# A two-layer graph network on one core: the second layer's preparation in new order, with an unused bf16 product ahead of each s product

## What is computed

```python
h = jnp.maximum(_layernorm(x), 0.0)
q, k, v = h @ Wq.T + bq, h @ Wk.T + bk, h @ Wv.T + bv
scores = jnp.where(adj > 0, q @ k.T / sqrt(128), neg)
x = x + jax.nn.elu(jax.nn.softmax(scores, axis=-1) @ v)

node = jnp.maximum(_layernorm(x), 0.0)
h = node @ W
s1, s2 = h @ a[:128, 0], h @ a[128:, 0]
e = jax.nn.leaky_relu(s1[:, None] + s2[None, :], negative_slope=0.01)
att = jax.nn.softmax(jnp.where(adj > 0, e, NEG_INF), axis=1)
x = x + h + att @ node
```

## Time and profile before

| | |
|---|---|
| median of three runs | 757.64 us (757.02 to 760.74) |
| profiled execution | 758.56 us, its span 756.7 us |
| mean granted TensorE clock | 0.977 |
| busy share: TensorE, VectorE, ScalarE, GpSimd | 95%, 74%, 72%, 59% |
| chain that ended last | TensorE's strip products 27%, ScalarE's signs 2.6%, one DMA 1.6% |
| layer one's last product of weights and v ends | 477.8 us |
| first strip of layer two starts | 510.9 us |

### The profile page before, as it was taken

How to read it: one execution, slowest core, us unless ns; L and a number is a source line. 1 busy time by engine, 2 the same in 40 slices (tenths; PEclk the granted TensorE clock), 3 DMA queues, 4 the chain that set the end, 5 groups by cost and what they waited for, 6 DMA issues and landing times. The chain is left out here.

```text
span 756.7 us, 18309 instructions
## 1 busy us (share of the span) xinstructions
PE 715.2 (95%) x6243; PEld 605.8 (80%) x6243; DVE 559.7 (74%) x1190; ACT 545.0 (72%) x1090; POOL 449.7 (59%) x388
## 2 busy tenths in 40 slices
PE   7989999999999999999999998759699999999996
PEld 5567888888888888888888787758588888888885
DVE  6977787887878788787878876679387477577572
ACT  4745877778687777878777787767986897887810
POOL 6687799999999999999999989480000000000000
PEclk9998999999999999999999999979899999999998
DMA  6289999998988889898888943963244342442100
GB/s 236 99 288 217 246 278 239 271 260 251 259 236 282 244 265 254 251 268 231 284 249 254 247 112 71 130 108 100 63 84 85 83 96 63 94 92 64 38 10 13
DMA packets 193307, 132.71 MB, mean 175 GB/s; under 512 B 174064, under 2 KB 180720, under 8 KB 184944
## 3 DMA queue, kind: packets, MB, share of 16 engines
q1 hardware_dynamic: 192528, 131.90, 65.7%
q10 hardware_dynamic: 576, 0.26, 0.1%
q0 software_dynamic: 160, 0.00, 0.0%
HBM read 71.31 MB, written 18.89 MB: 119 GB/s over the span
## 5 line engine op out<-in xcount | busy, mean ns | idle before, releaser
L770 ACT ACTIVATE scores<-scores,neg_max 128x1024 f32<-128x1024 f32 x128 | 146.0, 1142 | 50.5 <-DVE neg_max L904 50.5
L917 DVE TENSOR_TENSOR low<-scores 128x1024 bf16<-128x1024 f32 x96 | 138.1, 1438 | 39.2 <-ACT scores L770 39.2
L1171 PE MATMUL spare<-v_parts,hiT 128*128 128x256 bf16 x768 | 160.8, 273 | 0.0
L350 POOL TENSOR_SCALAR mask_both<-mask_bytes 128x2048 bf16<-128x2048 uint8 x64 | 153.2, 2394 | 5.4 <-POOL mask_bytes L345 0.4
L898 DVE CUSTOM_DVE_ANT_0 scores<-ps_s,mask_both 128x1024 f32<-128x1024 f32 x128 | 155.9, 1218 | 0.2 <-issue 0.2
L345 POOL TENSOR_SCALAR mask_bytes<-adj_both 128x2048 uint8<-128x2048 int32 x64 | 148.2, 2334 | 3.2 <-DMA adj_both<-in_adj 2.3
L1167 PE MATMUL spare<-v_parts,lowT 128*128 128x128 bf16 x768 | 144.1, 220 | 1.9 <-DMA lowT<-low 1.8
L784 ACT ACTIVATE hiT<-spare 128x512 bf16<-128x512 bf16 (+1 forms) x128 | 102.5, 801 | 39.2 <-PE spare L1141 36.7
L1605 PE MATMUL ps_x<-q_parts,over_k 128*128 128x258 bf16 x1024 | 117.0, 275 | 5.2 <-issue 4.0
L1605 PEld LDWEIGHTS ps_x<-q_parts,over_k 128*128 128x128 fp8e4 x1024 | 99.5, 98 | 20.7 <-issue 5.5
L1106 PE MATMUL ps_s<-k_hi,q_strip 128*128 128x512 f32 x256 | 112.6, 440 | 2.0 <-PEq L81 1.9
(11 more groups left out here) (174 smaller groups left out, 1274.4 us busy)
## 6 DMA issues: line engine op xcount, KB each, us to landing
adj_both<-in_adj SPq DMA_DIRECT2D x64, 1024.0 KB, 5.3
mask_bytes_dram<-mask_bytes SPq DMA_DIRECT2D x32, 512.0 KB, 2.8
x_sb<-in_x SPq DMA_DIRECT2D x8, 256.0 KB, 6.7
out<-res SPq DMA_DIRECT2D x32, 64.0 KB, 1.6
lowT<-low SPq DMA_TRANSPOSE x96, 4.8
mask_both<-s_row_dram SPq DMA_DIRECT2D x1, 1024.0 KB, 7.3
mask_both<-s_row_dram SPq DMA_DIRECT2D x1, 768.0 KB, 12.1
over_k<-mask_bytes_dram SPq DMA_TRANSPOSE x16, 4.6
```

The costliest lines, as they stand in the source:

```text
L350: return nc.gpsimd.tensor_scalar(out, src, -NEG, NEG, ALU.mult, ALU.add)
L770: nc.scalar.activation(sc, sc, ACT.Exp, bias=neg_max[:, bn:bn + 1], accum_out=row_sum[:, bn, k:k + 1]).then_inc(exp_done, 1)
L917: nc.vector.tensor_tensor(low[k][:], p, high_half(p), ALU.subtract).then_inc(low_done, 1)
L1171: last = nc.tensor.matmul(ps_a[:], high, v_parts[:, t, :, :], start=first, stop=final)
```

## The change

The diff does the following; only the end of the second block and the start of the third differ.

- `PIECES`: the tiles are prepared in nine pieces instead of eight chunks, the last two of two tiles each.
- GpSimd's `normalise` stands between its epilogues in another way: chunks 0 to 2 one strip later, 3 in the last one, 4 and 5 behind the last epilogue. VectorE takes the inverse root of tiles 24 to 29 and normalises them before the last epilogues are in, and does the same for 30 and 31 alone behind the last strip. In the last strip its low halves are made in another order.
- TensorE's s product of piece 0, the turn of piece 2 and the s1 product stand behind the strip's loop. Each s product of a tile has a product in front that nothing reads: `ident_half` (bf16 128 x 128) by 256 columns of `v_parts`, written to free columns of the s product's bank. There is a second s1 product (for strips 4 to 7), the order of hW products and turns is another, and the last three hW products stand behind `top_b`.
- ScalarE weighs nothing any more; VectorE weighs v1[0] of all chunks, GpSimd v1[1] of chunks 0 to 2 (`weigh_low`), and VectorE v1[1] of 3 to 7 at the start of the third block, where GpSimd splits them (`low_split`, for which strip 0 waits). VectorE makes the early signs of pieces 1, 3 and 5.
- SyncE issues the second `load_mask` before both `store_s1`; these hold chunks 2 to 4 and 5 to 7.
- The signs of group 1 are made from the second s1 product, 8 of them on VectorE (`VECTOR_SECOND`) and 24 on ScalarE, which waits for both transfers only for group 2. `add_last_hw` stands behind group 0.

The diff, cut to its core (indentation shortened):

```diff
+PIECES = [slice(4 * c, 4 * c + 4) for c in range(NC - 1)] + [slice(T - 4, T - 2), slice(T - 2, T)]
+NP2 = len(PIECES)
...
+def split_words(pool, c, i):
+halves = chunk(v1[i], c).bitcast(BF16)
+return nc.gpsimd.tensor_tensor(halves[:, :, 0::2], chunk(v1[i], c), halves[:, :, 1::2], ALU.subtract)
+def weigh_words(c, i):
+return nc.vector.scalar_tensor_tensor(out=v1[i][:, 4 * c:4 * c + 4, 0:D], in0=chunk(h_sb, c), scalar=0.0,
+                              in1=v1[i][:, 4 * c:4 * c + 4, D].unsqueeze(2).to_broadcast([D, 4, D]),
+                              op0=ALU.max, op1=ALU.mult)
...
-BY_SCALAR = (3, 4, 5, 6)
-S1_CHUNKS = (slice(1, 4), slice(4, NC))
+FIRST, MIDDLE, LAST = slice(0, 24), slice(24, 30), slice(30, 32)
+BY_VECTOR = (1, 3, 5)
+LOW_EARLY = 3
+S1_CHUNKS = (slice(2, 5), slice(5, NC))
...
+def pieces_till(c):
+return c + 1 if c < NC - 1 else NP2
...
 for b in range(4):
     load_mask(sp, 1, b, 1)
-store_s1(S1_CHUNKS[1], 1)
+for i, cs in enumerate(S1_CHUNKS):
+    store_s1(cs, i)
 @block.gpsimd
...
-    pool.wait_ge(weighed, c + 1)
-    if c in BY_SCALAR:
-        pool.wait_ge(weighed_by_scalar, BY_SCALAR.index(c) + 1)
-    for i in range(2):
-        halves = chunk(v1[i], c).bitcast(BF16)
-        nc.gpsimd.tensor_tensor(halves[:, :, 0::2], chunk(v1[i], c), halves[:, :, 1::2], ALU.subtract)
+def weigh_low(c):
+    pool.wait_ge(s_out, pieces_till(c))
+    for t in range(4 * c, 4 * c + 4):
+        last = nc.gpsimd.tensor_scalar(v1[1][:, t, 0:D], h_sb[:, t, :], 0.0, v1[1][:, t, D:D + 1],
+                                       ALU.max, ALU.mult)
+    last.then_inc(low_weighed, 1)
+    pool.wait_ge(low_weighed, c + 1)
+    split_words(pool, c, 1)
 def period(c, b):
     s = 4 * c + b
...
     if last_ones and s == T - 3:
         inverse_root(FIRST)
         pool.wait_ge(bytes_ready, 2 * T)
+    if last_ones and s == T - 2:
         for n in range(3):
             normalise(n)
-    if last_ones and s == T - 2:
-        for n in range(3, 6):
-            normalise(n)
+    if last_ones and s == T - 1:
+        normalise(3)
 all_periods(pool, period)
 add_elu(T - 2)
+normalise(4)
+normalise(5)
 for c in range(NC):
-    split_words(c)
+    pool.wait_ge(weighed, c + 1)
+    split_words(pool, c, 0)
+    if c < LOW_EARLY:
+        weigh_low(c)
 @block.scalar
...
+def early_signs(p):
+    act.wait_ge(s_out, p + 1)
     act.wait_ge(s1_out, 1)
-    for t in range(4 * c, 4 * c + 4):
+    for t in range(PIECES[p].start, PIECES[p].stop):
         last = sign_bytes(0, s1_row, t, EARLY)
-    if c == NC - 1:
+    if p == NP2 - 1:
         last.then_inc(signs_ready, 1)
-def weigh(c):
-    act.wait_ge(s_out, c + 1)
-    for t in range(4 * c, 4 * c + 4):
-        last = nc.scalar.activation(v1[0][:, t, 0:D], h_sb[:, t, :], ACT.Relu, scale=v1[0][:, t, D:D + 1])
-    last.then_inc(weighed_by_scalar, 1)
 all_periods(act, period)
 s_out_of(0)
-act.wait_ge(s1_made, 1)
-nc.scalar.activation(s1_row[:, 0:512], ps_s3[1], ACT.Copy).then_inc(s1_out, 1)
-hT_out(2)
 act.wait_ge(last_att, 1)
 act.wait_ge(epi_done, T - 1)
...
+hT_out(2)
+act.wait_ge(s1_made, 1)
+nc.scalar.activation(s1_row[:, 0:512], spare[2][:], ACT.Copy).then_inc(s1_out, 1)
 s_out_of(1)
 hT_out(3)
 early_signs(0)
-for c in range(2, NC):
-    s_out_of(c)
-    if c + 2 < NC:
-        hT_out(c + 2)
-    if c in BY_SCALAR:
-        weigh(c)
-    early_signs(c - 1)
-early_signs(NC - 1)
+for p in range(2, NP2):
+    s_out_of(p)
+    if p + 2 < NP2:
+        hT_out(p + 2)
+    if p - 1 not in BY_VECTOR:
+        early_signs(p - 1)
+early_signs(NP2 - 1)
+act.wait_ge(s1_made, 2)
+nc.scalar.activation(s1_row[:, 512:1024], ps_s3[1], ACT.Copy).then_inc(s1_out, 1)
 @block.vector
...
     if has(c, b, -1):
         inverse_sum(s - 1, (b + 3) % 4)
-    turned_low(s, 0)
-    low_part(s, b, 1)
     if ahead:
+        turned_low(s, 0)
+        low_part(s, b, 1)
         add_mask(s + 1, bn, 2)
-    turned_low(s, 1)
-    low_part(s, b, 2)
-    if ahead:
+        turned_low(s, 1)
+        low_part(s, b, 2)
         add_mask(s + 1, bn, 3)
         find_max(s + 1, bn)
+    else:
+        low_part(s, b, 1)
+        low_part(s, b, 2)
+        turned_low(s, 0)
+        turned_low(s, 1)
...
 inverse_sum(T - 1, 3)
 dve.wait_ge(epi_done, T - 2)
 moments_of(T - 3)
+aggregate(MIDDLE)
+add_eps(MIDDLE)
+inverse_root(MIDDLE)
+normalise(NC - 2)
+normalise(NC - 1)
 dve.wait_ge(epi_done, T - 1)
 moments_of(T - 2)
-aggregate(slice(LAST.start, T - 1))
+last_attention()
 weigh(0)
-last_attention()
-weigh(1)
 last_elu()
-aggregate(slice(T - 1, T))
+aggregate(LAST)
 add_eps(LAST)
 inverse_root(LAST)
-normalise(NC - 2)
-normalise(NC - 1)
-for c in range(2, NC - 1):
-    weigh(c)
-    if c >= 3:
-        add_hw(c - 3)
-dve.wait_ge(s_out, NC)
+normalise(NC)
+weigh(1)
+weigh(2)
+early_signs(1)
+weigh(3)
+early_signs(3)
+add_hw(0)
+weigh(4)
+add_hw(1)
+weigh(5)
+early_signs(5)
+add_hw(2)
+weigh(6)
+add_hw(3)
+dve.wait_ge(s_out, NP2)
...
-    if not ahead:
-        s_products(0)
-        nc.tensor.matmul(ps_s3[1], wa_rep[:], hT2[:, 0:512], start=True, stop=True).then_inc(s1_made, 1)
     if ahead2:
         make_scores(s + 2, b % 2, 0)
     turn_high(s, b, 2)
     times_v(s, 2)
     times_v(s, 3)
-    if not ahead:
-        turn_h(2)
...
-def s_products(c):
-    pe.wait_ge(hT_ready, c + 1)
-    wait(pe, s_out, c - 1)
-    for b in range(4):
-        last = nc.tensor.matmul(ps_s3[c % 2][:, 3 * b:3 * b + 3], hT2[:, 512 * c + D * b:512 * c + D * b + D],
+def s_products(p):
+    pe.wait_ge(hT_ready, p + 1)
+    wait(pe, s_out, p - 1)
+    for b, t in enumerate(range(PIECES[p].start, PIECES[p].stop)):
+        nc.tensor.matmul(ps_s3[p % 2][:, D:3 * D], ident_half[:], v_parts[:, 0, :, :], start=True, stop=True)
+        last = nc.tensor.matmul(ps_s3[p % 2][:, 3 * b:3 * b + 3], hT2[:, D * t:D * t + D],
                                 wa[:], start=True, stop=True)
     last.then_inc(s_made, 1)
...
 all_periods(pe, period)
+s_products(0)
 times_v(T - 1, 6)
 times_v(T - 1, 7)
-pe.wait_ge(s1_out, 1)
+turn_h(2)
+s1_product(0, spare[2][:])
 s_products(1)
 turn_h(3)
-for c in range(2, NC - 1):
-    s_products(c)
-    if c + 2 < NC:
-        turn_h(c + 2)
-    if c == 2:
+for p in range(2, NP2 - 1):
+    s_products(p)
+    if p == 2:
         pe.wait_ge(last_att, 1)
-    hw_product(c - 2)
-s_products(NC - 1)
-hw_product(NC - 3)
-hw_product(NC - 2)
-hw_product(NC - 1)
+    if 2 <= p < 6:
+        if p == 4:
+            pe.wait_ge(s1_out, 1)
+        hw_product(p - 2)
+    if p + 2 < NP2:
+        turn_h(p + 2)
+s_products(NP2 - 1)
+pe.wait_ge(s_out, NP2 - 1)
+s1_product(1, ps_s3[1])
 pe.wait_ge(top_ready, 1)
 nc.tensor.transpose(ps_s2[0:2, 0:D], top[:], ident[:])
 nc.tensor.matmul(ps_s2[:, D:2 * D], ones[:], hT_diag[:], start=True, stop=True).then_inc(top_t, 1)
+hw_product(4)
 pe.wait_ge(top_d, 1)
 nc.tensor.matmul(ps_s2[:, 0:2], ones[0:2, :], top_diag[:], start=True, stop=True).then_inc(top_b, 1)
+for c in range(5, NC):
+    hw_product(c)
...
+@block.gpsimd
+def _(pool):
+def fast(pool):
+    for n, c in enumerate(range(LOW_EARLY, NC)):
+        pool.wait_ge(weighed2, n + 1)
+        split_words(pool, c, 1).then_inc(low_split, 1)
+choose(pool, fast, lambda pool: None)
 @block.vector
 def _(dve):
...
+    for c in range(LOW_EARLY, NC):
+        weigh_words(c, 1).then_inc(weighed2, 1)
...
+        if isinstance(g, int) and g == 1 and b == 0:
+            dve.wait_ge(vector_second, 1)
...
     cut(0, 0, 3)
+    for t in range(VECTOR_SECOND):
+        last = compare_bytes(nc.vector, 1, s1_row[:, 512:1024], t, slice(0, 4))
+    last.then_inc(vector_second, 1)
     def result(g, par, b):
...
-            if isinstance(g, int) and g < 2:
-                act.wait_ge(s1_in[g], 16)
+            if isinstance(g, int) and g == 1:
+                for rows in s1_in:
...
             if more:
                 first_group = isinstance(g, int) and g == 0
-                for t in (range(16 * b - 16, 16 * b) if first_group else range(11 * b, 11 * b + 11)):
-                    if 0 <= t < T:
+                for t in (range(12 * b - 4, 12 * b + 8) if first_group else range(11 * b, 11 * b + 11)):
...
                 for t in range(T):
+                    if isinstance(s, int) and s == 0 and k == 1 and t % 4 == 0 and t // 4 >= LOW_EARLY:
+                        pe.wait_ge(low_split, t // 4 - LOW_EARLY + 1)
                     last = nc.tensor.matmul(ps_x[b % 2][k][:], by_key_tile(m, t)[:, b], v1[k][:, t, :].bitcast(BF16),
                                             start=(t == 0), stop=(t == T - 1))
```

80 lines of the change are left out of this document (43 added, 37 removed).

## The result

The changed kernel takes 751.71 us (median of 13 runs, 748.47 to 755.38), the kernel before in the same comparison 759.43 us (13 runs): a ratio of 0.9889, 95% interval 0.9865 to 0.9913, so 8.4 us faster (the two medians alone stand 7.7 apart). A second comparison gave 750.54 against 759.92, ratio 0.9877 (0.985 to 0.9903). The forecast was 744.3 with a range from 740 to 750: the sign was right, 13.8 us were forecast, and about 9 came. The forecast counted from 757.64 us for the kernel before, which took 759.43 in these 13 runs: so 1.8 of the 7.4 us between 744.3 and 751.71 are not the change's.

What follows compares the result with a forecast made beforehand. Bound: before strip 4 a chain through the s1-row transfer, ScalarE's signs and VectorE's cut, then TensorE alone. Gains 7.2 + 4.5 + 2.05 = 13.8 us gave 744.8 from 758.56, 743.8 from the median 757.64; forecast 744.3, range 740 to 750.

Steps and rivals of the forecast that it cites:

- 498.9 + 0.4 + 2.9 = 502.3: TensorE's end before strip 0: last small product at 498.9, then three hW products; strip 0 would start 7.2 us earlier.
- 20.1, so 499.6: covered: GpSimd before strip 0: 11 splits and 12 weighings take 20.1 us from 479.5, ending 499.6, hidden by under 3 us.
- 494.9: Last s values before strip 0 come at 494.9 us instead of 501.35.
- + 7.1: VectorE's tail behind the last s values: 8.2 us less one weighing of 1.07, ending at 502.0.
- Unused product at 0.11: Each unused 256-column product ahead of an s product costs TensorE 0.11 us, between 0.05 and 0.37.
- Strip 1 at P + 10.0: Strip 1 is free 10.0 us after strip 0 starts, behind VectorE's five weighings at 1.07 each and a cut.
- strip 4 at P + 31.9: Strip 4 starts 31.9 us after strip 0 instead of 36.45, by VectorE's list: 4.5 us gained.
- No long wait ahead of strip 4, 2.05 us not paid: From strip 4, the 2.05 us of half-speed products that followed the wait before it disappear.
- (1): Rival: VectorE's weighings and GpSimd's splits after strip 0's start take turns, +2.9 us, 747.2; chance 0.13.
- (2): Rival: the clock still falls before strip 0, over two pieces, +3.8 us, 748.1; chance 0.12.
- (3): Rival: unused products don't overlap, 0.37 us each, +8.3 less what ScalarE's pace hides, 751; chance 0.07.
- (4): Rival: unused products stop TensorE's stream; no gain from 0.53 us each, 764 us at 0.74; chance 0.03.

Runs made afterwards that it cites:

- e14: Changed kernel with 42 and 9 unused products put into TensorE's two waits ahead of the last three hW products; 749.23 us, ratio 0.9886 to the kernel before.
- e3: Changed kernel with hW products of chunks 4 to 6 ahead of TensorE's wait for the bound, chunk 7's in chunk 4's place; 748.23 us, again 748.67.
- after_again: The changed kernel itself, run again as yardstick; 750.54 us, ratio 0.9877 to the kernel before.
- e6: e3 with one group of strip 0's lower words split ahead of strip 0 instead of three; 751.71 us, ratio 0.9874 to the kernel before.
- e9: e3 with the early signs of piece 5 back on ScalarE instead of VectorE; 747.62 us, ratio 0.9837 to the kernel before; again 748.70.
- e11: Changed kernel with 46 and 22 unused products filling both gaps of TensorE's tail; 749.89 us, ratio 0.987 to the kernel before.
- e1: Changed kernel without the unused product ahead of each s product; 750.55 us, ratio 0.9875 to the kernel before.
- e4: Changed kernel with 36 unused products ahead of TensorE's wait for the sum of hT; 752.97 us, ratio 0.9889 to the kernel before.
- e7: Changed kernel in which ScalarE and VectorE wait for both s1 transfers before the signs of group 0; 752.87 us, ratio 0.9876 to the kernel before.
- e2: Changed kernel with four unused products ahead of each s product instead of one; 754.21 us, ratio 0.9912 to the kernel before.

## Why the prediction was wrong, by its own steps

**"498.9 + 0.4 + 2.9 = 502.3", the end of the stretch before P: the step that failed.** The three terms give 502.2, not 502.3. With M put at 458.85, as in the kernel before, the changed kernel ended it at 458.85 + 47.81 = 506.66. Of the 4.5 us from 502.2 to there, 1.8 are that the last small product came at M + 41.81 and not 40.05, because VectorE was late (below), and 2.7 are what TensorE did from there on, 6.0 us instead of 3.3. I had priced the three hW products at full speed. They stand behind two waits of TensorE, 5.00 and 1.33 us, and I had read in the kernel before that a gap of 3.35 us was followed by half speed. I applied that to the list up to 493 only, not to the tail. They took 5.49, and 2.94 in e14, where unused products keep the clock at 1.00 in the same order of work.

**"20.1, so 499.6: covered", GpSimd, too small by 5: the second step that failed.** It started at M + 19.80 (forecast 20.65) and ended at 45.78 instead of 40.75. Twelve weighings of a tile took 9.74 instead of 7.08, eleven splits 15.0 instead of 13.0, and 1.0 was a wait for VectorE. The shortest weighing is 0.71 and the shortest split 1.04; at these prices the list would take 8.5 + 11.4, close to my 20.1. The other 4.8 of the 24.8 is, by the turns shown above, time in which an instruction of GpSimd stood behind one of VectorE. I had taken prices from rows in which VectorE was partly idle; here it never is, and the two take turns. With TensorE's products repaired (e3, e14) this list binds, at P = M + 47.2. So of the 4.3 us that P came too late, the half clock is 2.0 (in after_again 1.2 of 3.5), and GpSimd the other 2.3: e6, which is e3 with two groups fewer on GpSimd's list and nothing else, has P at 44.83, where the forecast had 44.85. This is both engines' price: VectorE is last there, and ends at 43.46 instead of 44.87, since it too stands behind fewer splits; at 44.87 it would have put P near 46.2. The prediction named a GpSimd that ends last as what would make it wrong; here it was second.

**"494.9" and "+ 7.1", VectorE.** hT_total came at M + 36.64 (forecast 36.05), not because the s values were late, they came at 33.25, but because VectorE's own weighings, signs and sums took to then. I had looked at TensorE's and ScalarE's lists and at VectorE's only from the wait on. Its tail took 8.2 again, one weighing less, but its weighing, scaling and last half each stood behind a split. It ended at 44.87 instead of 43.15.

**Unused product at 0.11.** 0.045 for the first, 0.107 for each further one; the direction was right and nothing hung on it. The s product's four tiles took 1.0 us, not 1.26. att came at M + 17.68, forecast 18.75.

**Strip 1 at P + 10.0, strip 4 at P + 31.9.** P + 11.07 and P + 32.81. The five weighings took 5.64, 1.13 each, as forecast (1.07). The cut behind them took 4.8 instead of 3.6: its scaling and its lower half each waited for a split. From strip 1 on nothing waited: 21.74 for three strips. Strip 0 stopped twice for 0.83 for split words, but in e3, e9 and e11 it began at half clock and strip 1 still started at P + 11.08: that start hung on VectorE. In after_again, e1, e4 and e7 the clock fell to 0.50 in strip 1, and strips 1 to 3 took 23.11 us, 1.4 more; in the changed kernel's first profile, with the same three waits of 0.83, 0.83 and 1.72, it did not. So P to strip 4 is 34.15 to 34.19 in four of these five profiles, 2.3 us better than before and not 3.64. The prediction's sum has no term for these short waits. Why the clock held in one of the five stays open.

**No long wait ahead of strip 4, 2.05 us not paid: right.** The stretch from strip 4 on is 2.84 shorter. TensorE's part of it, up to where ScalarE takes the last sums, went from 203.13 to 201.13, so 2.0. The other 0.84 lie behind that, in the end of the program, 6.22 before and 5.38 after; the change touches nothing there, and the kernel before has one profile only.

**The rivals.** (1), weighing and splitting take turns, 0.13: the mechanism was right. A pair of them takes 1.45, not 1.66, and the first weighings go free, so that the five cost 5.64 and not 7.3; but I had looked for its price on these five alone, and it was paid on everything that the two engines do side by side: 4.8 us on GpSimd's list and 1.1 on VectorE's tail ahead of P, 1.2 on the cut. The rule of the Trainium skill, "SBUF — State Buffer", section "Who interferes with whom", that whoever issues first has the shared ports for its whole instruction and the other stands still, agrees with every row above on who waits, for tensor_scalar too; a pair takes 1.45 and not the 1.64 of the two alone (0.60 and 1.04), so that about 0.15 to 0.2 overlaps. I had set the rule aside for a mean of ten splits (0.15 more each), beside which VectorE had only a few weighings, and idle stretches. (2), the clock falls in stretch A anyway: the right mechanism in the wrong place, the s products, while it came on the tail. I had priced (1) and (2) one at a time; both came, in part. (3) and (4), dear unused products: 0.045 against 0.37 and 0.53.

## What to carry to other kernels

When a wait is removed, list what each engine does up to the same barrier, and add VectorE's and GpSimd's array work as if it ran in one line: here three lists ended within 3 us of each other, and repairing the last alone brought strip 0 forward by 1.0 to 2.0 us. Price TensorE's work behind a gap at the clock that the gap leaves, also where the gap is new because the work ahead of it became shorter. Put work that waits for nothing ahead of such a wait; here moving three products up (e3) put strip 0 at the same place as keeping the clock up with unused ones (e14).

## What was not expected of the hardware

- A bf16 product of 256 columns with its own weights, between float32 products of three columns, costs 0.045 us, and each further one 0.107 us.
- Turns hold for VectorE instructions with one array as input as well: hT_diag, 128 x 128, took 0.86 us behind a split and 0.28 to 0.29 without (e6, e2); a step on 128 x 2 values (L974) 1.07 where a split had begun with it. Adding TensorE's sums to an array (L347, 0.67 to 0.68 in every row) and copying them (L1128, 0.28) did not wait.
- In e11 all engines had ended by M + 46.48, and strip 0 began 4.0 us later, where 1.36 to 1.48 stood in every other kernel. The chain puts 3.42 us of that on no instruction. e14, with 17 unused products fewer, does not have it. I did not find the cause.
